# Four edits to a whole-network kernel: paired last columns in the experts, last deltas on VectorE, earlier `du` loads in the scan, a last stage begun tile by tile

## The reference

```python
# experts: each of 8 takes its 1024 best tokens; F = 682 = 5 * 128 + 42
mid = silu(tokens @ W_up[group] + b_up)
y   = zeros.at[idx].add(G * (mid @ W_down + b_down))
# selective scan
delta = softplus(dt_proj(dt))
state = exp(delta * A) * state + delta * Bm * uc        # over 1024 steps, 16 states
y = sum_n(state * Cm) ;  y = (y + uc * D) * silu(z) ;  x = x + y @ out_proj.T
# channel mix
xr = mu_r * x + (1 - mu_r) * x_prev ;  xk = mu_k * x + (1 - mu_k) * x_prev
out = sigmoid(xr @ W_r.T) * (relu(xk @ W_k.T) ** 2 @ W_v.T)
```

## Time and profile before

| | |
|---|---|
| median of 3 runs | 4936.78 us (4935.09 to 4944.33) |
| profiled execution, its own time | 4933.36 us |
| its span | 4931.6 us |
| TensorE matmuls busy | 4195.4 us (85%) |
| VectorE / ScalarE / GpSimd busy | 3070.1 / 2309.5 / 2409.9 us |
| granted TensorE clock, mean | 0.924 of full speed |

### The profile page before, as it was taken

The page is one execution under the profiler, slowest core; times in us unless marked ns, Lnnn a source line. Parts: engine busy times, 40 slices in busy tenths (PEclk is TensorE's granted clock), DMA queues, the critical chain, the costliest instruction groups (busy, mean ns, idle before and its releaser), DMA issues. The chain is left out here.

```text
span 4931.6 us, 117903 instructions
## 1 busy us (share of the span) xinstructions
PE 4195.4 (85%) x49696; PEld 2649.1 (54%) x49696; DVE 3070.1 (62%) x5364; ACT 2309.5 (47%) x3824; POOL 2409.9 (49%) x1569
## 2 busy tenths in 40 slices
PE   6399968699999996739997799879999999997798
PEld 5255545233333333625555544367777777875576
DVE  4511145687888884641116466479899899997574
ACT  1021124366666663101115367667667776763233
POOL 1034344222222223113432245479999899997553
...
GB/s 214 39 83 44 37 181 225 110 88 88 88 88 88 88 71 158 144 78 46 49 36 102 85 143 259 233 124 98 94 88 100 94 101 88 98 98 105 215 202 80
DMA packets 325609, 548.93 MB, mean 111 GB/s; under 512 B 55104, under 2 KB 221168, under 8 KB 325072
## 3 DMA queue, kind: packets, MB, share of 16 engines
...
...
## 5 line engine op out<-in xcount | busy, mean ns | idle before, releaser
L2331 POOL TENSOR_TENSOR s_hc<-s_hs,s_ct 128x1024 f32<-128x1024 f32 x512 | 1213.5, 2384 | 91.6 <-DVE s_hs L2310 77.1
L2310 DVE TENSOR_TENSOR_SCAN s_hs<-s_dA,s_psB 128x1024 f32<-128x1024 f32 x512 | 1167.3, 2285 | 126.3 <-PE s_psB L2244 63.8
L2244 PE MATMUL s_psB<-s_diag,s_duT 128*32 128x128 f32 x32768 | 962.7, 274 | 53.2 <-issue 28.2
L2244 PEld LDWEIGHTS s_psB<-s_diag,s_duT 128*32 128x32 f32 x32768 | 909.6, 111 | 157.5 <-issue 108.4
L1229 DVE CUSTOM_DVE_ANT_0 a_masked<-a_psM,a_later 128x1024 f32<-128x1024 f32 (+7 forms) x1024 | 734.0, 753 | 213.7 <-PE a_psM L1277 201.5
L1213 ACT ACTIVATE a_wt<-a_psE 128x512 f32<-128x512 f32 (+1 forms) x1216 | 627.4, 578 | 356.1 <-PE a_psE L1301 346.5
L2187 ACT ACTIVATE s_dA<-s_dlt,s_aneg 128x1024 f32<-128x1024 f32 x512 | 587.8, 1148 | 343.5 <-DVE s_hs L2310 339.6
L1192 POOL TENSOR_SCALAR_AFFINE_SELECT a_wt<-a_wt 128x512 f32<-128x512 f32 x256 | 162.3, 634 | 769.9 <-ACT a_wt L1213 769.9
L1277 PE MATMUL a_psM<-a_kst,a_qst 96*128 96x512 bf16 (+3 forms) x1536 | 421.8, 337 | 99.9 <-DVE a_mx L1229 68.0
L1301 PE MATMUL a_psE<-a_qst,a_kst 99*128 99x512 bf16 (+3 forms) x1536 | 413.7, 331 | 4.1 <-ACT a_wt L1213 2.4
L2167 ACT ACTIVATE s_diag<-s_ident,s_bt 128x128 f32<-128x128 f32 x972 | 322.2, 388 | 13.6 <-ACT s_ys L2176 13.5
...
...
## 6 DMA issues: line engine op xcount, KB each, us to landing
s_dlt<-dd SPq DMA_DIRECT2D x128, 512.0 KB, 4.5
...
```

The lines of the kernel that those rows point to most:

```text
L2244: ins = pe.matmul(psB[s][DG * m:DG * (m + 1), c * P:(c + 1) * P], duT[j % 2][:, c, DG * r:DG * (r + 1)], diag[:, place(NB * g + m, u), c, ...
L2310: dve.tensor_tensor_scan(hs[k % 2][:, :], dA[k % 2][:, :], psB[s][:, :], 0.0, ALU.mult, ALU.add).then_inc(scanned, 1)
L2331: pool.tensor_tensor(hc[NB * (g % 2) + r][:, :], hs[k % 2][:, :], ct[:, g, :], ALU.mult).then_inc(weighed, 1)
```

## The change

Four edits, one in each of four functions.

- `moe_ffn`: `up` of either half makes only its five full column tiles. After those of the odd half, the last 42 columns of both halves are made into one PSUM bank, the even half's in partitions 0 to 41 and the odd half's from partition 64 (`HI`), the two taken in turn within each `h`. ScalarE does both activations then; the odd half's `mid` tail, its `bu` and its `wdn` lie at partition 64 too, in `bu_hi` and `wdn_hi`, which SP loads besides (one load, and two for each expert). `down` waits for the new counts.
- `mamba_inputs`: `deltas` of batch 7 run on VectorE behind all its other work, with semaphores of their own.
- `mamba_scan`: the first `du` tile is loaded into `dA[1]`, third in SP's list, and turned from there. Later `du` loads go ahead of the tile's four `dlt` loads, or, in a batch's first tile, ahead of the fourth.
- `mamba_mix`: `o` of batch 0 runs tile by tile behind each gate, after four matmuls with zeros that open its banks. `o` of batch 1 moves behind k and r of batch 0; `t` of the next batch moves behind the first v and o. VectorE does `skips(1)` after the mix of batch 0 and `skips(2)` after the norm of batch 1. `g` is loaded for all four tiles as soon as `o` of two batches before is done.

```diff
+        def up_count(n, f):
+            e, u = n // 2, n % 2
+            return 2 * FT * e + (2 * (FT - 1) + u if f == FT - 1 else (FT - 1) * u + f) + 1
+        def place(n, f):
+            e, u = n // 2, n % 2
+            return ((2 * FT - 1) * e + (2 * (FT - 1) if f == FT - 1 else (FT - 1) * u + f)) % 4
+        def freed(n, f):
+            e, m = n // 2, (2 * (FT - 1) if f == FT - 1 else (FT - 1) * (n % 2) + f) - 4
+            return 2 * FT * e + m + 1 if m >= 0 else 2 * FT * (e - 1) + m + 2 * FT - 1 + (2 if m == -1 else 1)
         with nc.Block() as block:
...
+                sp.dma_start(bu_hi[HI:HI + FR, :], bup[0:FR, :]).then_inc(bu_loaded, 16)
...
-                                     (wdn[FR:FR + 1, e, FT - 1, :], bdown.rearrange("e (o d) -> e o d", o=1))):
+                                     (wdn[FR:FR + 1, e, FT - 1, :], bdown.rearrange("e (o d) -> e o d", o=1)),
+                                     (wdn_hi[HI:HI + FR, e, :], Wdown[:, (FT - 1) * P:F, :]),
+                                     (wdn_hi[HI + FR:HI + FR + 1, e, :], bdown.rearrange("e (o d) -> e o d", o=1))):
...
             def _(act):
                 act.wait_ge(ones_ready, 2)
-                act.wait_ge(bu_loaded, 16)
+                act.wait_ge(bu_loaded, 32)
+                def inner(n, f):
+                    u, grp = n % 2, n // (2 * GS)
+                    act.wait_ge(up_ready, up_count(n, f))
+                    lo, r = (HI, FR) if f == FT - 1 and u else (0, FR if f == FT - 1 else P)
+                    bias = bu_hi[lo:lo + r, grp * FT + f:grp * FT + f + 1] if lo else bu[0:r, grp, f:f + 1]
+                    act.activation(mid[u][lo:lo + r, f, :], psU[place(n, f)][lo:lo + r, :], ACT.Silu, bias=bias).then_inc(mid_ready, 1)
                 for n in range(NT):
-                    u, grp = n % 2, n // (2 * GS)
                     if n >= 2:
                         act.wait_ge(down_ready, 2 * (n - 1))
-                    for f in range(FT):
-                        r = P if f < FT - 1 else FR
-                        act.wait_ge(up_ready, FT * n + f + 1)
-                        act.activation(mid[u][0:r, f, :], psU[(FT * n + f) % 4][0:r, :], ACT.Silu,
-                                       bias=bu[0:r, grp, f:f + 1]).then_inc(mid_ready, 1)
+                    for f in range(FT - 1):
+                        inner(n, f)
+                    if n % 2:
+                        inner(n - 1, FT - 1)
+                        inner(n, FT - 1)
...
                     pe.wait_ge(wup_loaded[grp], 16)
-                    for f in range(FT):
-                        r, m = P if f < FT - 1 else FR, FT * n + f
-                        if m >= 4:
-                            pe.wait_ge(mid_ready, m - 3)
+                    for f in range(FT - 1):
+                        if freed(n, f) > 0:
+                            pe.wait_ge(mid_ready, freed(n, f))
                         for h in range(DH):
-                            ins = pe.matmul(psU[m % 4][0:r, :], wup[:, grp, h, f * P:f * P + r], gT[u][:, h, :],
+                            ins = pe.matmul(psU[place(n, f)][:, :], wup[:, grp, h, f * P:(f + 1) * P], gT[u][:, h, :],
                                             start=(h == 0), stop=(h == DH - 1))
                         ins.then_inc(up_ready, 1)
+                    if u:
+                        pe.wait_ge(mid_ready, freed(n, FT - 1))
+                        for h in range(DH):
+                            for v in range(2):
+                                ins = pe.matmul(psU[place(n, FT - 1)][HI * v:HI * v + FR, :], wup[:, grp, h, (FT - 1) * P:F],
+                                                gT[v][:, h, :], start=(h == 0), stop=(h == DH - 1))
+                                if h == DH - 1:
+                                    ins.then_inc(up_ready, 1)
                 def down(n):
                     e, u = n // 2, n % 2
-                    pe.wait_ge(mid_ready, FT * (n + 1))
-                    pe.wait_ge(wdn_loaded[e], 48)
+                    pe.wait_ge(mid_ready, 2 * FT * e + 2 * FT - 1 + u)
+                    pe.wait_ge(wdn_loaded[e], 16 * 5)
                     for k in range(2):
                         if n:
                             pe.wait_ge(y_ready, 2 * (n - 1) + k + 1)
                         for j in range(2):
                             t = 2 * k + j
                             for f in range(FT):
-                                r = P if f < FT - 1 else FR + 1
-                                ins = pe.matmul(psD[k][:, j * D:(j + 1) * D], mid[u][0:r, f, t * P:(t + 1) * P],
-                                                wdn[0:r, e, f, :], start=(f == 0), stop=(f == FT - 1))
+                                lo, r = (HI * u, FR + 1) if f == FT - 1 else (0, P)
+                                wd = wdn_hi[lo:lo + r, e, :] if lo else wdn[0:r, e, f, :]
+                                ins = pe.matmul(psD[k][:, j * D:(j + 1) * D], mid[u][lo:lo + r, f, t * P:(t + 1) * P],
+                                                wd, start=(f == 0), stop=(f == FT - 1))
                         ins.then_inc(down_ready, 1)
...
+        def summed(b):
+            return dl_ready if b < B - 1 else dl_last
+        def multiplied(b):
+            return du_ready if b < B - 1 else du_last
+        def made(b, j):
+            return IT_ * b + j + 1 if b < B - 1 else j + 1
+        def deltas(eng, b, j):
+            n = IT_ * b + j
+            eng.wait_ge(ln_ready, n + 1)
+            eng.wait_ge(pos_ready, n + 1)
+            eng.tensor_tensor(dl[b % 2][j][:, :], pos[j][:, :], dl[b % 2][j][:, :], ALU.add).then_inc(summed(b), 1)
+            eng.wait_ge(summed(b), made(b, j))
+            if n >= NDU:
+                eng.wait_ge(du_stored[n % NDU], 16 * (n // NDU))
+            eng.tensor_tensor(du[n % NDU][:, :], dl[b % 2][j][:, :], uc[b % 2][:, j, :], ALU.mult).then_inc(multiplied(b), 1)
...
+                    deltas(dve, B - 1, j)
...
+                sp.dma_start(dA[1][:, :], dud[0][0:P, :]).then_inc(first_loaded, 16)
...
-                        if j == 0 and not last:
+                        more = j < IT_ - 1 or not last
+                        rows_first = j == 0 and not last
+                        if rows_first:
                             hold(sp, turned, TURNS * b + 2, passed)
                             sp.dma_start(du[0:NS, :], bcd[b + 1][0:NS, :]).then_inc(du_loaded, 16)
-                        if j < IT_ - 1 or not last:
+                        elif more:
+                            inputs(b + (j + 1) // IT_, (j + 1) % IT_, TURNS * b + turn_count(j + 1, last))
+                        if more:
                             for k in range(NB):
+                                if rows_first and k == NB - 1:
+                                    inputs(b, 1, TURNS * b + turn_count(1, last))
                                 hold(sp, scanned, SCANNED0 + UPB * b + s + 3 * k, passed)
                                 deltas(b + (j + 1) // IT_, (j + 1) % IT_, k)
-                        if j < IT_ - 1 or not last:
-                            inputs(b + (j + 1) // IT_, (j + 1) % IT_, TURNS * b + turn_count(j + 1, last))
...
-                sp.wait_ge(turned, 1)
-                sp.dma_start(du[:, :], dud[0][0:P, :]).then_inc(du_loaded, 16)
...
+                def turn_u(s, src):
                     for c in range(NC):
-                        ins = pe.transpose(psB[s][:, c * P:(c + 1) * P], du[:, c * P:(c + 1) * P], ident[:, :])
+                        ins = pe.transpose(psB[s][:, c * P:(c + 1) * P], src[:, c * P:(c + 1) * P], ident[:, :])
...
+                            loads = TURNS * b + turn_count(x, last)
+                            if x:
+                                hold(pe, du_loaded, 16 * loads, passed)
+                                turn_u(s, du)
+                            else:
+                                turn_b(s, loads)
...
-        USES = [(b, kind, k) for b, kind in ((0, "o"), (0, "t"), (1, "o")) for k in range(4)]
+        USES = [(0, kind, k) for kind in "ot" for k in range(4)]
         for b_ in range(B):
             USES += [(b_, kind, k) for kind in "kr" for k in range(4)]
-            USES += [(b_ + 1, "t", k) for k in range(4) if b_ + 1 < B]
+            USES += [(1, "o", k) for k in range(4) if b_ == 0]
             for k in range(4):
                 USES += [(b_, "v", k)]
                 USES += [(b_ + 2, "o", k)] if b_ + 2 < B else []
+                USES += [(b_ + 1, "t", h) for h in range(4) if k == 0 and b_ + 1 < B]
         order_of = {use: i for i, use in enumerate(USES)}
...
                         sp.wait_ge(xo_ready, 4 * (b - NX + 1))
+                    if b >= 2:
+                        sp.wait_ge(o_ready, 4 * (b - 1))
+                    if b:
+                        for j in range(IT_):
+                            sp.dma_start(g[b % 2][:, j, :], yd[b][j * P:(j + 1) * P, :]).then_inc(g_loaded[b % 2][j], 16)
```

(31 more changed lines are left out.)

35 lines of the change are left out of this document (15 added, 20 removed).

## The result

The changed kernel takes 4851.30 us (median of 4 runs, 4846.81 to 4853.17) against 4940.12 before (the three runs of above and one more): a ratio of 0.982 with a 95% interval of 0.980 to 0.984. It is 1.8% faster, which is clear of the noise; 4860 was predicted. The profiled execution took 4846.8 (span 4845.1) against 4933.4.

What follows compares the result with a forecast made beforehand. No engine was taken to bound the whole kernel; each edit was priced by what ends last in its stage. 27.6 + 8.2 + 23 + 18.8 = 77.6 off 4933.4 gave 4855.8, 4860 as a median, range 4843 to 4885.

Steps and rivals of the forecast that it cites:

- Bound by stage: Whole kernel: no engine bounds all of it, so each edit is priced against what ends last in its stage.
- Experts: Expert stages: paired 42-column passes overlap fully, 1.95 us a block; gain 30.6 less 3 for down, -27.6 us (0 to -31).
- Last deltas: End of mamba_inputs: eight instructions move from GpSimd to idle VectorE, taking 10.1 us; -8.2 us (-5 to -9).
- Scan, opening: Start of mamba_scan: first du load lands earlier, VectorE's blocks then decide the first scan; -3.1 us (-1 to -3.5).
- Scan, inside: Later du turns in mamba_scan: earlier loads save 23.8 us of VectorE's waits, of which 4 go back to ScalarE.
- Last stage, periods: mamba_mix, per batch: new order shortens the spacing of keys from 41.3 us to T+37.2; five periods give -20 us.
- last batch: mamba_mix, last batch: v(6,0) now stands before t(7), so keys(7) come 1.7 us later.
- Last stage, opening: Start of mamba_mix: o(0) ends earlier, but TensorE idles nearly 20 us before o(2,0); k(1) nearly unmoved, -0.5 us.
- (a): Expert stages: the paired passes run in series, so the experts give 0; 4888 us, chance 0.06.
- (b): Scan: ScalarE takes over the late turns, so only 10 of 23 us stay; 4873 us, chance 0.15.
- (c): Last stage: gates come later than T+16.4 or the opening's hole is longer, so it gives nothing; 4879 us, chance 0.13.
- (d): Scan: TensorE's instructions arrive late, 2.88 us at each of 32 early du loads, net +14; 4951 us, chance 0.04.

Runs made afterwards that it cites:

- the pair of runs above: Changed kernel with the halves' last 42 columns issued one half after the other, 4848.28 us; then with both halves in the same array columns, 4876.10 us.
- the run with the order alone: Kernel before with one edit: in the last stage, t of the next batch stands behind the first v and o; 4913.61 us against 4934.88, ratio 0.996.

## Why the prediction was right

- **Bound by stage.** Each term was priced in its own stage, and the five stages carry 84.6 of 86.5 us. That held.
- **Experts, -27.6 (measured -27.9; -29.3 by the mean of the fourteen stages).** Full overlap, 1.95 us a block (1.92), shown by the pair of runs above. The 3 us for `down` were 1.6: it waits once a stage, at the last expert, not 0.1 at each. That the passes must alternate was my belief after the result, and fell.
- **Last deltas, -8.2 (-8.7).** Eight instructions took 9.7 us where 10.1 were counted, and the stores gave back 0.6. A slip of the sum made no difference: at 423 GB/s a megabyte (two stores of 512 KB) takes 2.5 us, not 2.6.
- **Scan, opening, -3.1 (-1.0 at the first scan).** This step failed. It took VectorE's blocks and one exponential for next late, and left out ScalarE's list, in which 32 blocks stand ahead of the copy of `duT`, and the 3.8 us of TensorE behind that copy. (Its own terms give 3239.4, where it wrote 3239.6.) By unit 4 the profile has -3.6, but the other runs with this opening reach 0.9 to 4.0 there: TensorE's stop after 208 passes decides, and with it the time at which the instructions land.
- **Scan, inside, -20 (-26.1; -25.5 against the mean of eight).** This is the term that was off by most, and it was too small. The runs give 14.4 for the batch ends and 9.0 for the rest, 23.4, where 16.8 and 7, less 4, were counted. The mechanism and the 4 given back were right. Two things were sized too small. Of the four batch ends that only looked like TensorE's I counted 0.5 us each; by the starts of the scans units 60 to 64 of batches 0, 2, 4 and 6 took 44.1 us before (41.7 in the run with the order alone, whose scan is the same) and 38.9 after, 0.7 to 1.3 each. And units 4 to 12, for which no gain was counted, took 171.2 and 172.0 us in the two runs with the scan of before and 168.3 to 170.7 in the eight with the changed one.
- **Last stage, periods, -20 (-19.5), last batch +1.7 (+1.0).** Right, with 0.9 us of wait for the gates where 0.8 was predicted (its rows give 16.4 - 15.7 = 0.7).
- **Last stage, opening, -0.5 (-2.4).** The hole was foreseen within a us (nearly 20; 19.3), and the sum lies within its bounds. With U the end of o(1), the start of k(1) was foreseen at about U+44 and measured at U+44.3, but the terms that the prediction writes out reach only U+42.2; the difference is the slow o(2,0) behind the hole. gates(2) began at U+8.3, not at U+11.7 (the prediction's first come, first served gives 8.1), but took 12.5 us in all, so they ended at U+20.8 where 21.4 was predicted. What the prediction did not see is that the first period gains by the order too, and that the opening's own edits therefore lose 1.1 to 2.5 us.
- **Rivals.** (a) and (b) are refuted by runs. (c) by the periods. (d) by the scan's waits: TensorE's stalls for nothing that the list of waits shows came to 28.2 us before and to 19.5 now. In the scan's opening it is at work: there the late instructions ate what an earlier first scan would have given.
- **Luck.** It had a small part. The sum was 7.0 us short of the 84.6; the scan's opening, 2.1 too much, and the periods, 0.5 too much, hid a little of what the other terms lacked.
